# Two transformer layers on one core: layer 1's cross attention laid out anew and joined with its MLP in one loop

## The reference, cut to what matters

```python
# layer 1: 16 heads of 16
xn, yn = layernorm(x), layernorm(context)
q = xn @ Wq                      # (8, 512, 256)
k, v = split(yn @ Wkv)           # (8, 64, 256) each
o = softmax(q k^T / 4) v         # per head, over the 64 context tokens
x = x + (o @ Wproj + bproj)
x = x + (gelu(layernorm(x) @ W1 + b1) @ W2 + b2)     # hidden 1024
# layer 2: 16 heads of 64
x = selfattention(layernorm(x)) + x
x = crossattention(layernorm(x), context) + x
x = geglu(layernorm(x)) + x
```

## Time and profile before

| | us |
|---|---|
| median of 3 runs | 2549.8 (2546.5 to 2552.2) |
| the profiled execution | 2542.1 |
| its span, first to last instruction | 2540.3 |
| layer 1's attention, with what precedes its loop | 130 to 461 |
| layer 1's MLP | 461 to 678 |
| layer 2's self attention begins | 685 |
| layer 2's cross attention with MLP | 1962 to 2541 |

### The profile page before, as it was taken

The page is one execution under the profiler, slowest core; times in us unless marked ns, Lnnn a source line. Parts: engine busy times, 40 slices in busy tenths (PEclk is TensorE's granted clock), DMA queues, the critical chain, the costliest instruction groups (busy, mean ns, idle before and its releaser), DMA issues.

```text
span 2540.3 us, 30663 instructions
## 1 busy us (share of the span) xinstructions
PE 2187.3 (86%) x11372; PEld 1784.2 (70%) x11372; DVE 1729.9 (68%) x2402; ACT 1189.5 (47%) x1760; POOL 1215.6 (48%) x1034
## 2 busy tenths in 40 slices
PE   6637877799779999999999999999998699999998
PEld 4425655688667777777777777777776578888886
DVE  5547776465578777777777777777776567776653
ACT  5413333222246665666566566655664334444431
POOL 2027676222236556556565665656555544443322
PEclk9858898999889999999999999999999899999999
DMA  6920111112100010000000000000013422221000
GB/s 218 361 74 31 61 60 46 56 51 75 40 17 22 14 34 14 22 22 18 30 14 22 26 13 30 14 26 22 14 36 117 165 95 83 83 83 75 9 9 17
DMA packets 78068, 140.89 MB, mean 55 GB/s; under 512 B 29216, under 2 KB 36768, under 8 KB 75872
## 3 DMA queue, kind: packets, MB, share of 16 engines
q1 hardware_dynamic: 77920, 138.93, 15.7%
HBM read 87.52 MB, written 50.86 MB: 54 GB/s over the span
## 4 chain that ended last, share of the span: by engine, by line
PE 37%; DVE 19%; POOL 15%; issue 14%; ACT 11%; DMA 3%; SPq 0%; POOLq 0%; DVEq 0%; ACTq 0%
PE PS L151 10%; PE PS L153 9%; PE PS L152 9%; DVE R L167 8%; POOL R L164 8%; ACT R L161 5%; PE PS L1238 3%; DVE F L1453 2%; ACT F L161 2%; POOL R L170 2%; PE PS L1242 2%; PE PS L1275 2%; ACT F L1374 2%; POOL F L1532 2%; PE PS L157 1%
## 5 line engine op out<-in xcount | busy, mean ns | idle before, releaser
L151 PE MATMUL PS<-R 128*128 128x256 f32 (+1 forms) x2900 | 1031.0, 356 | 186.9 <-DVE R L167 82.5
L152 PE MATMUL PS<-R 128*128 128x256 f32 (+1 forms) x2900 | 999.7, 345 | 0.0
L153 PE MATMUL PS<-R 128*128 128x256 f32 (+1 forms) x2900 | 998.4, 344 | 0.0
L164 POOL TENSOR_SCALAR R<-F 128x1024 fp32r<-128x1024 f32 (+1 forms) x519 | 575.5, 1112 | 519.9 <-DVE F L1778 238.1
L151 PEld LDWEIGHTS PS<-R 128*128 128x128 f32 x2900 | 560.0, 193 | 318.7 <-DVE R L167 84.4
L167 DVE TENSOR_TENSOR R<-F,R 128x1024 fp32r<-128x1024 f32 (+2 forms) x476 | 620.6, 1310 | 148.6 <-POOL R L164 143.3
L161 ACT ACTIVATE R<-PS 64x512 fp32r<-64x512 f32 (+4 forms) x820 | 454.7, 566 | 373.2 <-PE PS L153 185.3
L153 PEld LDWEIGHTS PS<-R 128*128 128x128 f32 x2900 | 560.6, 193 | 65.8
L152 PEld LDWEIGHTS PS<-R 128*128 128x128 f32 x2900 | 561.7, 194 | 58.7
L1374 ACT ACTIVATE F<-PS 128x1024 f32<-128x1024 f32 x256 | 263.1, 1028 | 329.1 <-PE PS L1242 205.5
L1453 DVE TENSOR_REDUCE F<-PS 128x2 f32<-128x1024 f32 x256 | 303.6, 1217 | 5.5 <-PE PS L1275 4.7
(11 more groups left out here) (69 smaller groups left out, 1686.5 us busy)
## 6 DMA issues: line engine op xcount, KB each, us to landing
gd<-R SPq DMA_DIRECT2D x8, 2048.0 KB, 6.6
vd<-R SPq DMA_DIRECT2D x8, 2048.0 KB, 8.1
F<-sd SPq DMA_DIRECT2D x128, 128.0 KB
R<-gd SPq DMA_DIRECT2D x8, 2048.0 KB, 8.4
R<-vd SPq DMA_DIRECT2D x8, 2048.0 KB, 8.3
xs<-F SPq DMA_DIRECT2D x24, 512.0 KB, 2.6
F<-xs SPq DMA_DIRECT2D x24, 512.0 KB, 3.5
F<-in_x SPq DMA_DIRECT2D x8, 512.0 KB, 3.7
```

Of the source, the lines that this page charges most:

```text
L151: nc.tensor.matmul(o, L[0], Rr[0], start=start, stop=False, skip_group_check=share)
L152: nc.tensor.matmul(o, L[0], Rr[1], start=False, stop=False, skip_group_check=share)
L153: return nc.tensor.matmul(o, L[1], Rr[0], start=False, stop=stop, skip_group_check=share)
L164: return nc.gpsimd.tensor_scalar(o, i, 1.0, 1.0, ALU.mult, ALU.mult)
```

## The change

Layer 1 gets the form of layer 2's cross attention. Iteration `i` of one loop of 43 handles 128 tokens and all 16 heads (`N0` = 32 of them), and from `i` = 10 on also two steps of the MLP of earlier tokens (`LAG0` = 10). The masks, the selector, the second set of scores, the matmul that subtracts the largest, the way of the sums through memory, the store and the loads between attention and MLP are gone. Keys are laid on the diagonal of a zeroed tile by eight DMAs a batch (`keys`). Values are written into a zeroed tile by four small copies a batch, and their rests by four more. The output of 256 tokens is computed in odd iterations, its projection in even ones, the query of the next batch when i%4 is 3. The normalizations of layer 1 (`norm0`: for attention when i%4 is 2, for the MLP when i%4 is 0 from 8 on) are scaled by four ACTIVATEs with scale and bias from columns (`ln_scale_act`), for which VectorE computes `shift`; their transposes go to banks 0 and 1. GpSimd splits them and adds the bias. The weights of `w1` and `w2` are copied by ScalarE and their rests taken by GpSimd. The next stage's weights are loaded and split from i = 34 on. Context loads come first on SyncE's queue, and buffers of x are numbered anew.

```diff
+        def ln_scale_act(k, src):
+            act.wait_ge(ln_shift, k - 1)
+            act.wait_ge(ln_nl, k - 1)
+            for q in range(4):
+                m = act_copy(xt[:, q, :], src[:, q, :], scale=rstd[:, q:q + 1], bias=shift[:, q:q + 1])
+            m.then_inc(ln_unit.sem, 1)
+        def ln_shift_dve(k):
+            dve.wait_ge(ln_rstd, k)
+            nc.vector.scalar_tensor_tensor(out=shift, in0=mv[:, :, 0], scalar=-1.0, in1=rstd, op0=ALU.mult, op1=ALU.mult
+                                           ).then_inc(ln_shift.sem, 1)
...
+            KT, Q1 = ra.take(2, 2, NT), ra.pair(2, NT)
+            yn = ra.pair(2, NT)
+            VB = [ra.take(1168) for _ in range(2)]
+            PT1 = ra.pair(8, 256)
+            OT1 = ra.pair(512)
+            h1 = [ra.pair(NT) for _ in range(3)]
+            ns1 = [ra.pair(2, NT) for _ in range(2)]
+            stage1 = fa.take(3 * 1024)
+            E1 = [stage1[:, 1024 * i:1024 * i + 1024] for i in range(3)]
+            X1 = [X0[0], *(fa.take(4, C) for _ in range(3)), X0[1]]
+            w12_stage = fa.take(3 * 512)
+            hf1 = [w12_stage[:, 512 * i:512 * i + 512] for i in range(3)]
+            brow1 = fa.take(C)
+            kd_b = [shaped(slot[3], 2048 * i, (2, 2, NT)) for i in range(2)]
...
+        g2 = jobs_of(("w1", "w2"), w12_stage, 1)
+        g3 = jobs_of(("k1", "q1", "v1"), stage1, 2)
...
+        N0, NM, LAG0 = 4 * NB, 8 * NB, 10
+        loop0 = range(N0 + LAG0 + 1)
...
+            kind = "x" if i % 4 == 2 else "g" if i % 4 == 0 and i >= 8 else "s" if i == N0 + 7 else None
+            b = {"x": i // 4 + 1, "g": i // 4 - 2, "s": 0, None: NB}[kind]
+            if b < NB:
+                norm0[i] = kind, b, 2 + len(norm0)
...
+            def keys(b):
+                for h in range(8):
+                    rows = slice(16 * h, 16 * h + 16)
+                    nc.sync.dma_start(f32(kd_b[b % 2])[rows, :, :, 64 * h:64 * h + 64],
+                                      f32(KT)[rows, :, :, 64 * b:64 * b + 64]).then_inc(k0_in[b % 2].sem, 16)
...
+            def query(b):
+                pe.wait_ge(ln_nl, number0["x", b])
+                wait_weights(pe, "q")
+                pe.wait_ge(sc0_sub, 4 * b - 1)
+                for g in range(2):
+                    for k in range(2):
+                        m = mm3(bank(g), [v[:, k, 128 * g:128 * g + 128] for v in W0q], [v[:, k, :] for v in ns[b % 2]],
+                                k == 0, k == 1)
+                    m.then_inc(q0_mm.sem, 1)
...
+            def turn(c, half):
+                pe.wait_ge(p0_mul, c)
+                pe.wait_ge(t0_lo, 2 * c + half - 1)
+                for k in range(4):
+                    pr = 4 * half + k
+                    m = nc.tensor.transpose(bank(2)[:, 128 * k:128 * k + 128], E1[c % 3][:, 128 * pr:128 * pr + 128], ident)
+                m.then_inc(t0_mm.sem, 1)
+            def scores(c):
+                b, q = divmod(c, 4)
+                pe.wait_ge(q0_lo, 2 * b + 1)
+                pe.wait_ge(k0_in[b % 2], b // 2)
+                pe.wait_ge(sc0_sub, c - 1)
+                if c - 1 in norm0:
+                    pe.wait_ge(ln_aff, 2 * norm0[c - 1][2] + 1)
+                for g in range(2):
+                    m = mm3(bank(g), [v[:, g, 128 * q:128 * q + 128] for v in Q1], [kd_b[b % 2][:, hl, g, :] for hl in range(2)],
+                            True, True)
+                m.then_inc(sc0_mm.sem, 1)
+            def output(m_):
+                pe.wait_ge(t0_lo, 4 * m_ + 3)
+                pe.wait_ge(v0_lo, m_ // 2)
+                pe.wait_ge(o0_add, m_ - 1)
+                for g in range(2):
+                    for k in range(4):
+                        pr = 4 * g + k
+                        m = mm3(bank(3)[:, 256 * g:256 * g + 256], [v[:, 128 * pr:128 * pr + 128] for v in VB],
+                                [v[:, pr, :] for v in PT1], k == 0, k == 3)
+                m.then_inc(av0_mm.sem, 1)
+            def project(m_):
+                pe.wait_ge(o0_lo, m_)
+                wait_weights(pe, "proj")
+                for q in range(2):
+                    for g in range(2):
+                        m = mm3(bank(3)[:, 256 * q:256 * q + 256],
+                                [v[:, 256 * g + 128 * q:256 * g + 128 * q + 128] for v in OT1], [v[:, g, :] for v in W0p],
+                                g == 0, g == 1)
+                m.then_inc(o0_mm.sem, 1)
...
+            def down(n):
+                b, m_ = divmod(n, 8)
+                pe.wait_ge(h_lo, n)
+                wait_weights(pe, "w2")
...
+            value(0)
+            query(0)
+            for i in loop0:
+                c, n = i - 2, 2 * (i - LAG0)
+                if ok(c, N0):
+                    turn(c, 0)
+                if ok(i, N0):
+                    scores(i)
+                if ok(c, N0):
+                    turn(c, 1)
+                if ok(n, NM):
+                    up(n)
+                if ok(n - 1, NM):
+                    down(n - 1)
+                if i % 4 == 3 and ok(i // 4 + 1, NB):
+                    query(i // 4 + 1)
+                if i % 2 == 1 and ok((i - 3) // 2, 2 * NB):
+                    output((i - 3) // 2)
+                if i % 2 == 0 and ok((i - 4) // 2, 2 * NB):
+                    project((i - 4) // 2)
+                if i in norm0:
+                    pe.wait_ge(sc0_sub, min(i, N0 - 1))
+                    ln_transpose(norm0[i][2], 0)
+                if ok(n + 1, NM):
+                    up(n + 1)
+                if i % 4 == 2 and ok((i - 2) // 4, NB) and i > 2:
+                    value((i - 2) // 4)
+                if ok(n, NM):
+                    down(n)
...
+            for i in loop0:
+                c, n = i - 2, 2 * (i - LAG0)
+                if ok(c, N0):
+                    turned(c, 0)
+                    turned(c, 1)
+                if ok(i, N0):
+                    act.wait_ge(sc0_sub, i)
+                    nc.scalar.activation(E1[i % 3], E1[i % 3], ACT.Exp, scale=0.25).then_inc(e0.sem, 1)
+                for job in weights0_at(i):
+                    act_weight(job)
+                if i in norm0:
+                    kind, b, k = norm0[i]
+                    ln_scale_act(k, xbuf(norm0_at[kind][0], b))
+                if ok(n, NM):
+                    gelus(n)
+                if i % 4 == 3 and ok(i // 4 + 1, NB):
+                    query(i // 4 + 1)
+                if i % 2 == 1 and ok((i - 3) // 2, 2 * NB):
+                    m_ = (i - 3) // 2
+                    act.wait_ge(av0_mm, m_)
+                    act.wait_ge(o0_mm, m_ - 1)
+                    act_copy(OT1[0], bank(3)).then_inc(o0_hi.sem, 1)
+                if i in norm0:
+                    ln_affine(k, norm0_at[kind][1], norm0_at[kind][2], 0)
+                if ok(n + 1, NM):
+                    gelus(n + 1)
+                if i % 4 == 2 and ok((i - 2) // 4, NB) and i > 2:
+                    value((i - 2) // 4)
...
+            def differences(c):
+                dve.wait_ge(sc0_max, c)
+                dve.wait_ge(w_lo_pool, [j.rest for j in g1 if j.by_pool][-1])
+                dve.wait_ge(t0_mm, 2 * (c - 3) + 1)
+                nc.vector.tensor_tensor(heads(E1[c % 3]), heads(bank(0, 2)), mx4.unsqueeze(2).to_broadcast([128, 16, 64]),
+                                        ALU.subtract).then_inc(sc0_sub.sem, 1)
...
+            for i in loop0:
+                c, n = i - 2, 2 * (i - LAG0)
+                if ok(c, N0):
+                    turned(c, 0)
+                if ok(n - 1, NM):
+                    rests(n - 1)
+                if ok(i - 1, N0):
+                    sums(i - 1)
+                if i in norm0:
+                    ln_shift_dve(norm0[i][2])
+                if ok(i, N0):
+                    largest(i)
+                if ok(c, N0):
+                    turned(c, 1)
+                if ok(i, N0):
+                    differences(i)
+                if ok(n, NM):
+                    rests(n)
+                if n >= 8 and n % 8 == 0:
+                    b = n // 8 - 1
+                    dve.wait_ge(down_mm, n - 1)
+                    dve.wait_ge(x_bias, number0["g", b] - 1)
+                    for k in range(2):
+                        xv = X1[b % 5][:, 2 * k:2 * k + 2, :]
+                        nc.vector.tensor_tensor(xv, bank(6 + k).rearrange("p (a c) -> p a c", a=2), xv, ALU.add
+                                                ).then_inc(res.sem, 1)
+                if i % 4 == 3 and ok(i // 4 + 1, NB):
+                    query(i // 4 + 1)
+                if i % 2 == 1 and ok((i - 3) // 2, 2 * NB):
+                    dve.wait_ge(o0_hi, (i - 3) // 2)
+                    dve_rest(OT1[1], bank(3), OT1[0]).then_inc(o0_lo.sem, 1)
+                if i % 2 == 0 and ok((i - 4) // 2, 2 * NB):
+                    b, half = divmod((i - 4) // 2, 2)
+                    dve.wait_ge(o0_mm, 2 * b + half)
+                    dve.wait_ge(x_bias, number0["x", b] - 1)
```

(41 more changed lines are left out.)

753 lines of the change are left out of this document (215 added, 538 removed).

## The result

The changed kernel takes 2604.77 us (median of four executions, 2602.48 to 2612.39) against 2548.69 (2546.52 to 2552.2): a ratio of 1.0224, 95% interval 1.02 to 1.0248. It is slower, by 56 us, where I had forecast slower by 17. The profiled executions are 2612.39 us (span 2610.6) against 2542.1.

The account below looks back on a forecast made before the run. A chain through the engines, not TensorE's issue, bounds the loop. Prologue to 166, lead-in 99, combined 338 and tail 82 give 685 us, +3 at the next stage; clock +14 gives +17, 2559.1 profiled, 2567 as median; range 2518 to 2595.

Parts of the forecast that it names:

- Combined iterations: Loop i = 10 to 31, attention with MLP: 62.5 us for four iterations, 338 us in all.
- down(n) waits for h_lo(n): End of the iteration's chain: TensorE's last block waits for VectorE's rest; 12.7 us with nothing added.
- The clock: TensorE at half clock after gaps: 8 us for half of ten norm iterations, 6 for the lead-in, +14.
- Plain and query iterations: Combined iterations without a norm: 12.9 us at i%4 = 1, 15.4 us at i%4 = 3.
- The stalled rest: Norm iterations: VectorE's rest beside GpSimd's bias addition lasts 2.88 instead of 0.69 us, 2.2 more.
- Lead-in: Iterations i = 0 to 9, attention alone: 99 us, bounds 90 and 108, plus 6 for the clock.
- Prologue: Up to the first scores: these start at 166 instead of 183.3 us, -17, bounds -12 to -20.
- Tail: After i = 31: 11.6 and 10.5 us, then 18 MLP steps at 3.3, and 1: 82 us.
- The third: Rival: slower, the clock falls in the whole loop, some 35 us more, 2600 us; chance 0.1.
- The first: Rival: faster, TensorE sets the pace, 12.1 us an iteration, 267 instead of 338, about 2496 us; chance 0.1.
- The second: Rival: chains too long by a microsecond an iteration and the clock holds, 2531 to about 2553 us; chance 0.3.
- The fourth: Rival: keys' small packets late or x buffers wait for stores, +3 to 7 a batch, 2590 to 2620; chance 0.02.

Follow-up runs that it names:

- e4: Changed kernel with the first layer's GELU replaced by the identity of the same shape, removing the table loads: 2580.0 us.
- e1: Changed kernel with value(b) behind down(n) in TensorE's queue in iterations i%4 = 2: 2606.6 us.
- e6: Changed kernel with the two residual additions (res, o0_add) ahead of rests(n) in VectorE's queue: 2593.8 us.
- e8: Changed kernel with nine unread 128x512 matmuls added behind up(n + 1) in the ten combined norm iterations: 2598.9 us.
- e3: Changed kernel with the norms inside the loop scaled by VectorE behind differences, not by ScalarE: 2583.4 us.
- e10: Changed kernel with e5, e6 and, for i < N0 alone, e2 joined, value one iteration later, norms still scaled by ScalarE: 2571.6 us.
- e5: Changed kernel with slot 3 cleared ahead of the first norm's power, and output with its copies ahead of the query: 2595.3 us.
- e12: e11 with the transposes of the tail's two norms behind down(n) and their affine copies behind the second GELU: 2528.8 us.
- e11: Changed kernel with e3, e5, e6 and, for i < N0 alone, e2 joined, value in its old place behind up(n + 1): 2519.7 us.
- e2: Changed kernel with GpSimd's addition of the bias to x behind rounds(n + 1): 2592.9 us.

## Why the prediction was wrong, point by point

- **Direction and mechanism** were right: the loop is bound by a chain through four engines, TensorE is relieved of nothing, and alternating exponent and GELU puts a table load on the chain (e4; not in the iteration with the query). The size was wrong: 2567 against 2604.8, above the range's 2595.
- **Combined iterations, +27.5 us: the step that failed is "down(n) waits for h_lo(n)", with nothing else beside it.** In the iteration i%4 = 2 it also waits for `res`, and `value`, ahead of it in TensorE's queue, for `o0_add`; both additions stand behind the stalled rest. I had named neither addition and had counted `value` only in TensorE's issue. 1.28 + 0.68 + 1.0 for `value` at full clock is 3.0 us in each of five iterations and 1.7 in i = 10, which has no `res`: some 16.5. Of these i = 30 has no norm, and I had it at 12.7; it took 17.9. e1 showed that there are two waits, e6 that they are the cause: with both additions early, i = 10 to 31 takes 20 us less.
- **The clock**: the mechanism was right, the share was mis-sized. I took half clock in half of the ten norm iterations; it was in all ten and in i = 30. Down(n) took 2.7 and 2.6 us for 1.54 in e6, `value` 1.7 for 1.0 in e8: 1.1 x 11 + 0.7 x 6 = 16.3 against 8. With the 16.5 above this gives 25 of the 27.5; the rest lies scattered over the other iterations.
- **Plain and query iterations** (12.9 and 15.4): measured 13.0 and 15.5. **ScalarE's scaling** (2.0): measured 2.06. **The stalled rest** (2.2 more): 2.83 for 0.69. **"The ln_scale that VectorE no longer does buys nothing"**: right, e3 and e10. **The load** before the exponent is hidden: right, e4.
- **Lead-in, +4**: the pairs with a norm took 29.8 and 30.6 us where I had 26.5 and 27, because TensorE idles 4 to 7 us ahead of the transposes and then runs the transposes (1.94 us for eight, 1.06 elsewhere) and the query (0.43 us a matmul) at half clock. Of the 10.7 us that e3 gets back, 6.5 are the scaling; I read the rest as clock. The pair without a norm missed by more, 17.7 for 13.7 (i = 4 and 5): behind a wait of 2.43 us for VectorE's rest its output ran at half clock, 5.3 us from 224.96 where I had 2.9. The two other pairs took 8.8 for 10 and 22.2 for 21.6.
- **Prologue, +3.5**: two lengths that I took from the old prologue failed. `ln_scale` took 4.40 us and not 1.25 beside GpSimd's clearing of slot 3, which the change puts there. But without the clearing (e5) only 0.8 us arrives, because VectorE's statistics of x, which wait for x, stand ahead of the context's rests: these end 18.0 us behind the context's DMA, 17.2 in e5, where my walk had 14.4. The walk also left 0.5 us between the query and the first scores, where its copy and rest took 1.6. The keys on the diagonal cost nothing, as forecast: their sixteen DMAs are issued from 160.31 to 171.03, and the first scores wait for VectorE's rest, not for them.
- **Tail, +10**: I took the old MLP's 3.3 us a step, norms included. Without a norm a step is 2.82 us, as before. But three steps with a norm take 16.2 us (GELUs at 690.88 and 707.11) and not 8.5, and two such norms fall in the tail. What holds them is not settled: in e12 later transposes made the tail longer, not shorter; with VectorE scaling instead of ScalarE, which idles 5.1 us ahead of its scaling there, e11 still has 118.0. GpSimd's addition, split and roundings and VectorE's rest beside them are my guess, since e2 and e12 both lengthen the tail by delaying them; no run cleared it, and it is not shown.
- **Rivals.** The third (2600, the clock falls in the whole loop) comes nearest in time but not in mechanism: the clock was 0.89. The first, TensorE's pace of 12.1 us, was not reached even when both norm iterations had come down to 12.9. The second named e2's effect rightly (2.2 us from each norm iteration); the chains were too short by far more. The fourth did not occur.
- My range left out the case in which a norm iteration has a second wait. I had asked of every added instruction what it costs, but not of every wait in the written order what stands ahead of its releaser.

## What to carry to other kernels

Go through every wait of a hand-written order, those at a batch's first block too, and look in the releasing engine's queue at what stands ahead of the release: two additions behind a stalled subtraction, with `value` behind them, cost 3.0 us an iteration, more than any single step that I had counted (2.0 for the scaling, 2.2 for the stall). Clear all engines' queues around one point together, since the cuts are worth more than one by one: e2, e3, e5 and e6 gain 9 to 21 us each, 54 in sum, and together 85 (e11). Some 10 of the difference is the loss in the tail that e2 has and e11 avoids. Another part is the clock, which the closed gaps keep up: for the same 1531 matmuls TensorE's busy time falls from 264 to 239 us. Work on an idle engine, here VectorE between `differences` and the rest, is free where the same work on the engine that carries the chain costs its whole length twice a batch.
